# Contexts of a second attention formed transposed on four column groups, in a kernel of two gated layers

## What is computed

```python
x = x + tanh(g_xattn[0]) * L0_xattn(ctx, norm(x), mask, ...)    # 16 heads of 64, over 77 + 128 keys
x = x + tanh(g_ffn[0])   * L0_ffn(norm(x), ...)                 # 128 -> 512, butterflies, gelu, 512 -> 128
x = x + tanh(g_xattn[1]) * L1_xattn(norm(x), ctx, ...)          # 16 heads of 8, the 32 best of 77 keys
x = x + tanh(g_ffn[1])   * L1_ffn(norm(x), ...)                 # 8 experts, the best one for each token
```

```python
scores = einsum('bhsd,bhnd->bhsn', Q, K) / SCALE
topk_scores, topk_indices = top_k(scores, 32)
weights = softmax(topk_scores)
context = einsum('bhsk,bhskd->bhsd', weights, selected V)       # 8 values a head, 16 heads
out = context @ Wo.T + bo
```

## Time and profile before

| | us |
|---|---|
| median of 3 executions | 827.6 |
| lowest and highest | 823.84, 827.65 |
| the profiled execution | 824.25 |
| its span, first to last instruction | 822.5 |
| busy in the span: PE, DVE, ACT, POOL | 727.6, 594.8, 460.3, 453.1 |

### The profile page before, as it was taken

How to read it: one execution, slowest core, us unless ns; L and a number is a source line. 1 busy time by engine, 2 the same in 40 slices (tenths; PEclk the granted TensorE clock), 3 DMA queues, 4 the chain that set the end, 5 groups by cost and what they waited for, 6 DMA issues and landing times.

```text
span 822.5 us, 17993 instructions
## 1 busy us (share of the span) xinstructions
PE 727.6 (88%) x4442; PEld 579.1 (70%) x4442; DVE 594.8 (72%) x3758; ACT 460.3 (56%) x1226; POOL 453.1 (55%) x705
## 2 busy tenths in 40 slices
PE   6789989799999999999999999999999967763796
PEld 5556666677777777777777777777776845552696
DVE  2745435678888888888888888888887888994132
ACT  2265557476858575767676676758575724221231
POOL 6265735755556565655657565656575544653144
PEclk9899999999999999999999999999999965555799
DMA  7200099910000000000000000000000000100772
GB/s 190 60 1 1 8 313 310 293 51 1 1 2 1 0 0 0 0 0 0 0 0 0 0 0 0 0 0 0 0 1 1 2 0 1 39 33 33 202 217 78
DMA packets 38531, 37.85 MB, mean 46 GB/s; under 512 B 3632, under 2 KB 34247, under 8 KB 38482
## 3 DMA queue, kind: packets, MB, share of 16 engines
q1 hardware_dynamic: 32984, 27.76, 12.3%
q10 hardware_dynamic: 3994, 6.36, 2.6%
q0 software_dynamic: 1504, 3.17, 1.1%
HBM read 16.28 MB, written 21.45 MB: 46 GB/s over the span
## 4 chain that ended last, share of the span: by engine, by line
PE 51%; DVE 23%; issue 9%; POOL 6%; ACT 5%; SPq 3%; DMA 2%; DVEq 0%; another core or an unknown queue 0%; POOLq 0%; ACTq 0%
DVE raw L1533 9%; PE bank L850 9%; PE bank L722 8%; DVE m L1527 6%; PE bank L877 4%; PE bank L867 4%; PE bank L868 4%; PE bank L838 4%; PE bank L919 3%; PE bank L936 3%; DVE negmax L1475 3%; PE bank L1156 3%; PE bank L1166 2%; ACT prob L1184 2%; PE bank L899 2%
## 5 line engine op out<-in xcount | busy, mean ns | idle before, releaser
L1533 DVE MATCH_REPLACE8 raw<-m,raw 128x77 f32<-128x77 f32 x1024 | 220.0, 222 | 0.0
L1527 DVE MAX8 m<-raw 128x8 f32<-128x77 f32 x1024 | 189.1, 225 | 1.1 <-DVE raw L1533 0.6
L1184 ACT ACTIVATE prob<-bank,negmax 128x205 f32<-128x205 f32 x256 | 108.3, 428 | 129.1 <-DVE negmax L1475 128.7
L514 POOL TENSOR_TENSOR raw<-raw,m 128x616 f32<-128x616 f32 x64 | 77.9, 1217 | 143.4 <-DVEq L1509 143.4
L495 POOL TENSOR_TENSOR prob<-prob,inv 128x820 f32<-128x820 f32 x64 | 99.4, 1554 | 72.6 <-DVE inv L1480 72.6
L850 PE MATMUL bank<-kvT,g_sb 128*128 128x205 f32 x512 | 123.4, 364 | 0.0
L1475 DVE TENSOR_REDUCE negmax<-bank 128x2 f32<-128x410 f32 x128 | 74.0, 578 | 50.6 <-PE bank L850 49.6
L850 PEld LDWEIGHTS bank<-kvT,g_sb 128*128 128x128 f32 x512 | 82.6, 189 | 10.1
L936 PEld LDWEIGHTS bank<-v,p1T 77*128 77x128 f32 x512 | 75.1, 217 | 15.1 <-issue 4.7
L936 PE MATMUL bank<-v,p1T 77*128 (+1 forms) x512 | 72.4, 269 | 8.1 <-ACT p1T L1184 3.9
L1533 DVE MATCH_VALUE_LOAD raw<-m,raw 128x8 f32 x1024 | 77.7, 76 | 0.0
(11 more groups left out here) (232 smaller groups left out, 1347.6 us busy)
## 6 DMA issues: line engine op xcount, KB each, us to landing
z_sorted<-no_row SPq DMA_DIRECT2D x1, 17415.0 KB, 64.4
b_w<-in_L_ffn_W ACTq DMA_DIRECT2D x23, 256.0 KB, 3.2
z_tile<-z_sorted SPq DMA_DIRECT2D x23, 129.0 KB, 3.2
w<-in_L_ffn_W SPq DMA_DIRECT2D x8, 256.0 KB, 4.6
raw<-in_L_xattn_Wkv SPq DMA_DIRECT2D x2, 512.0 KB, 5.5
xs<-in_x SPq DMA_DIRECT2D x1, 960.0 KB, 6.9
cx<-in_ctx SPq DMA_DIRECT2D x1, 577.5 KB
raw<-in_L_xattn_Wq SPq DMA_DIRECT2D x1, 512.0 KB, 3.7
```

Source lines behind the costliest of these rows:

```text
L1184: return nc.scalar.activation(dst, src, f, **kw)
L1527: v.max(m8[:, h, r, :], sw[:, h, src, :]).then_inc(s[name], 1)
L1533: v.match_replace(sw[:, h, 1, :], m8[:, h, r, :], sw[:, h, src, :], TAKEN)\
```

## The change

The values are held without the column of ones; for each batch GpSimd (`widen_values`, slot 4) copies them into `v_wide`, in which a block of 32 columns holds the 8 values of one head and zeros. The contexts of a batch are formed all at once, in slot 1 of E, and transposed: the weights are 32 columns of v_wide or of `ones_wide`, the moving operand is p1T of one head (now kept for all 16), and head 4j + q is summed into the rows 32j to 32j + 31 of the result (its own 8 rows there, zeros in the others), by the j-th group of 32 columns of TensorE. The ones give the sums, spread over the same rows. So 32 products of 32 weight columns and 128 moving columns take the place of 16 of 128 weight columns and 9 moving ones, and c_zT comes from VectorE directly: the reciprocal is of 128x128, and context_T with its copy is gone. Users of bank X stand further apart in slots 3 to 5 of TensorE and ScalarE. spread_keys goes from slot 0 to slot 2 of GpSimd, and the last roots are taken in three parts, in slot 6 of step 2 and slots 2 and 6 of step 3. TensorE's loop starts at step 5.

```diff
 k1T = sb("k1T", [128, NB, NK])
-v1 = sb("v1", [NK, NB, H, D1 + 1])
+v1 = sb("v1", [NK, NB, H, D1])
+v_wide = sb("v_wide", [NK, QUADS * (128 + D1)])
+ones_wide = sb("ones_wide", [NK, QUADS, 32])
 wr = sb("wr", [128, NE])
...
 m8 = sb("m8", [128, H, ROUNDS, 8])
-p1T = sb("p1T", [NK, 4, 128])
-c_inv = sb("c_inv", [128, H])
-c_z = sb("c_z", [128, H, D1])
+c_inv = sb("c_inv", [128, 128])
 c_zT = sb("c_zT", [128, 128])
...
-z_tile = flat("z_tile", RING * ROW).rearrange("p (u w) -> p u w", u=RING)
+z_flat = flat("z_tile", RING * ROW)
+z_tile = z_flat.rearrange("p (u w) -> p u w", u=RING)
+p1T = z_flat[0:NK, 2 * ROW:2 * ROW + H * 128].rearrange("p (h q) -> p h q", h=H)
 bf_rows = z_tile[0:2 * PST * HC, 0, 0:256]
...
            topk_done=8, sub_done=4, e_done=4, p1_ready=4, p1T_psum=4, p1T_ready=4,
-           ctx_psum=4, cinv_ready=1, cz_ready=1, cT_psum=1, cT_ready=1, o1_psum=1, xo_added=1,
+           ctx_psum=1, vw_ready=1, cinv_ready=1, cz_ready=1, o1_psum=1, xo_added=1,
            x3_ready=1, c_stats=2, c_eps=1, crs_ready=1, rz_ready=1, rz_kept=1, rT_psum=1, rT_ready=1,
...
     g.iota(token_no[:, :], pattern=[[128, NB]], base=0, channel_multiplier=1).then_inc(s["c_token"], 1)
-    g.memset(v1[:, :, :, D1:D1 + 1], 1.0).then_inc(s["c_const"], 1)
-    pool.wait_ge(s["c_const"], 6 + NE)
+    for w in (v_wide[:, :], ones_wide[:, :, :]):
+        g.memset(w, 0.0).then_inc(s["c_const"], 1)
+    pool.wait_ge(s["c_const"], 7 + NE)
+    for q in range(QUADS):
+        g.memset(ones_wide[:, q, D1 * q:D1 * q + D1], 1.0).then_inc(s["c_const"], 1)
     g.affine_select(out=ident[:, :], in_=ident[:, :], compare_op=ALU.not_equal, fill=1.0, base=0,
...
-    def roots(b0, b1):
+    def roots(b0, b1, parts=(0, 1, 2)):
...
         rx, rx2, rc, exponent = (a[:, b0:b1] for a in (rs_x, rs_x2, rs_c, half))
-        pool.wait_ge(s["st_x"], 2 if b1 == 1 else 2 * NB)
-        then(g.tensor_scalar(rx, var_x, EPS, 1.0, ALU.add, ALU.mult))
-        then(g.tensor_tensor(rx, rx, exponent, ALU.pow))
-        then(g.tensor_tensor(rx2, rx, rx, ALU.mult))
-        then(g.tensor_tensor(rx2, rx2, var_x, ALU.mult))
-        then(g.tensor_scalar(rx2, rx2, EPS, 1.0, ALU.add, ALU.mult))
-        pool.wait_ge(s["st_c"], 2 if b1 == 1 else 2 * NB)
-        then(g.tensor_scalar(rc, var_c, EPS, 1.0, ALU.add, ALU.mult))
-        then(g.tensor_tensor(rc, rc, exponent[0:NK, :], ALU.pow))
-        then(g.tensor_tensor(rx2, rx2, exponent, ALU.pow))
-        then(g.tensor_tensor(rx, rx, rx2, ALU.mult))
+        if 0 in parts:
+            pool.wait_ge(s["st_x"], 2 if b1 == 1 else 2 * NB)
+            then(g.tensor_scalar(rx, var_x, EPS, 1.0, ALU.add, ALU.mult))
+            then(g.tensor_tensor(rx, rx, exponent, ALU.pow))
+        if 1 in parts:
+            then(g.tensor_tensor(rx2, rx, rx, ALU.mult))
+            then(g.tensor_tensor(rx2, rx2, var_x, ALU.mult))
+            then(g.tensor_scalar(rx2, rx2, EPS, 1.0, ALU.add, ALU.mult))
+            then(g.tensor_tensor(rx2, rx2, exponent, ALU.pow))
+            then(g.tensor_tensor(rx, rx, rx2, ALU.mult))
+        if 2 in parts:
+            pool.wait_ge(s["st_c"], 2 if b1 == 1 else 2 * NB)
+            then(g.tensor_scalar(rc, var_c, EPS, 1.0, ALU.add, ALU.mult))
+            then(g.tensor_tensor(rc, rc, exponent[0:NK, :], ALU.pow))
...
                         ALU.mult).then_inc(s["kbd_ready"], 1)
+
+    def widen_values(b):
+        reach(pool, "ctx_psum", b, 0)
+        w = v_wide[:, :].rearrange("p (q r) -> p q r", q=QUADS)[:, :, 0:128]
+        g.tensor_copy(w.rearrange("p q (j w) -> p q j w", j=4)[:, :, :, 0:D1],
+                      batch(v1.rearrange("p b h d -> p b (h d)"), b).rearrange("p (j q d) -> p q j d", q=QUADS, j=4))\
+            .then_inc(s["vw_ready"], 1)
...
                     rsqrt(B, b_mv, b_rs, "b_stats", "b_eps", "brs_ready")
-                    spread_keys(B)
             if slot == 1:
...
                     copy_keys(A)
+                if B is not None:
+                    spread_keys(B)
             if slot == 3:
...
                     keep_top(C, 2)
+                    widen_values(C)
                 if P is not None:
...
                 roots(1, 4)
-            if (i, slot) == (3, 6):
-                roots(4, NB)
+            if (i, slot) in ((2, 6), (3, 2), (3, 6)):
+                roots(4, NB, {(2, 6): (0,), (3, 2): (1,), (3, 6): (2,)}[i, slot])
             if slot == 5:
...
-    def contexts(b, q):
+    def contexts(b):
         free("M")
-        reach(pe, "p1T_ready", b, q + 1)
-        for n in range(4):
-            c = CT0 + (4 * q + n) * (D1 + 1)
-            last = mm(M[:, c:c + D1 + 1], p1T[:, n, :], v1[:, bass.ds(b, 1), 4 * q + n, :].squeeze(1),
-                      start=True, stop=True)
+        reach(pe, "p1T_ready", b, QUADS)
+        reach(pe, "vw_ready", b, 1)
+        for q in range(QUADS):
+            for n in range(2):
+                for j in range(4):
+                    w = v_wide[:, 128 * q + 32 * j:128 * q + 32 * j + 32] if n == 0 else ones_wide[:, q, :]
+                    last = mm(M[32 * j:32 * j + 32, CT0 + 128 * n:CT0 + 128 * n + 128], w, p1T[:, 4 * j + q, :],
+                              start=(q == 0 and n == 0), stop=(q == QUADS - 1), skip_group_check=True)
         last.then_inc(s["ctx_psum"], 1)
-        if q == QUADS - 1:
-            read_next("M", "cz_ready", 5, 1)
-
-    def context_T(b):
+        read_next("M", "cz_ready", 5, 1)
+
+    def second_out(b):
         free("M")
         reach(pe, "cz_ready", b, 1)
-        turn(M[:, 0:128], c_z[:, :, :].rearrange("p h d -> p (h d)")).then_inc(s["cT_psum"], 1)
-        read_next("M", "cT_ready", 5, 1)
-
-    def second_out(b):
-        free("M")
-        reach(pe, "cT_ready", b, 1)
         mm(M[:, 0:D], c_zT[:, :], l1_wT[:, 3, :], start=True, stop=True).then_inc(s["o1_psum"], 1)
...
                     scores(A, 2)
-                if C is not None:
-                    contexts(C, 0)
                 if B is not None:
...
                     project_out(A2, 3)
-                if E is not None:
-                    context_T(E)
                 if A is not None:
                     project(A, 2)
-                    probs_T(A, 0)
+                if C is not None:
+                    second_probs_T(C, 1, 4)
                 if E is not None:
...
                 if A is not None:
+                    probs_T(A, 0)
                     scores(A, 3)
-                if C is not None:
-                    second_probs_T(C, 1, 4)
             if slot == 4:
-                if A is not None:
-                    attend(A, 0, 1)
-                if A is not None:
-                    scores(A, 4)
                 if B is not None:
                     second_scores(B, 0)
-                if C is not None:
-                    contexts(C, 1)
+                if A is not None:
+                    attend(A, 0, 1)
+                if A is not None:
+                    scores(A, 4)
                 if B is not None:
...
                     probs_T(A, 1)
+                if C is not None:
+                    second_probs_T(C, 2, 4)
+                if A is not None:
                     project(A, 3)
...
                     ffn_T(A2)
-                if C is not None:
-                    second_probs_T(C, 2, 4)
                 if A is not None:
                     scores(A, 5)
+                if B is not None:
+                    second_scores(B, 2)
                 if E is not None:
                     router_T(E)
-                if B is not None:
-                    second_scores(B, 2)
             if slot == 6:
...
                     scores(A, 6)
-                if C is not None:
-                    contexts(C, 2)
                 if A is not None:
...
                 if E is not None:
-                    if i == 5:
-                        pe.wait_ge(s["ld_router"], 32)
                     logits(E)
...
-    run_steps(pe, step)
+    def before_loop():
+
+        pe.wait_ge(s["ld_router"], 32)
+        free("M")
+        read_next("M", "lg_ready", 6, 2)
+
+    run_steps(pe, step, LAGS - 1, before_loop)
...
             if slot == 3:
-                if E is not None:
-                    move(E, c_zT, "cT_psum", "cT_ready")
                 if A is not None:
                     projected(A, 2)
+                if C is not None:
+                    second_probs_out(C, 1)
+                if A is not None:
                     probs_out(A, 0)
                     exps(A, 3)
-                if C is not None:
-                    second_probs_out(C, 1)
                 if i == 2:
...
             if slot == 4:
-                if A is not None:
-                    attended(A, 0)
                 if B is not None:
                     second_scores_out(B, 0)
+                if A is not None:
+                    attended(A, 0)
                 if C is not None:
...
                     probs_out(A, 1)
+                if C is not None:
```

(49 more changed lines are left out.)

## The result

| | before | after |
|---|---|---|
| median, us (4 executions each) | 825.8 | 835.8 |
| lowest to highest | 823.8 to 827.7 | 833.8 to 837.3 |
| the profiled execution, its span | 824.25, 822.5 | 834.4, 832.5 |
| TensorE busy in the span | 727.6 | 703.0 |
| loop step, down to down | 38.78 | 39.66, but 41.2 in four of ten |

The account below looks back on a forecast made before the run. TensorE and VectorE were taken to bound the kernel in turn, VectorE pacing slots 0 to 4. 11 x 1.1 - 3.5 - 2 - 1 + 1.5 = +7 on 824.25 gave 831; forecast 833 us, range 829 to 843.

Parts of the forecast that it names:

- Spreading to slot 2: GpSimd's product moved away from b_z: b_z falls from 2.28 to 0.34 us, first maxima start 1.2 us earlier.
- Contexts: TensorE, slot 1: 64 records on four column groups take 2.1 us, between 1.8 and 7.1, replacing 3.2.
- rival (b): Weight loads on TensorE are not covered by streaming: contexts take 3.5 us, kernel 855 us; chance 0.12.
- VectorE's wait: Slot 1: VectorE waits 1.1 us for the contexts, where it waited nothing before.
- Reciprocal: On VectorE, grown from 128x16 to 128x128: 953 ns against 240, +0.71 us.
- Maxima of slots 2 and 4: VectorE: slot 2 maxima at 395.3 against 394.67, 0.6 late; slot 4 maxima at 406.0 against 405.44.
- TensorE's wait for the copy of scores (B,1): Ahead of second_probs_T(C,2), TensorE waits 1.2 us for bank X; slot 5 maxima 1.15 late, +1.1 us a step.
- Start, roots, sort step and end: Outside the 11 full steps: first steps -3.5, roots -2, sort constants -1, last step +1.5 us.
- waits 1.2 us: TensorE's forecast wait ahead of second_probs_T(C,2) for ScalarE to free bank X, if today's place is kept.
- my number stands: If b_z stays slow, maxima 1 at 390.8 still come before the contexts end, so the forecast is unchanged.
- wherever it is earlier, it waits longer: If second_probs_T(C,2) stands earlier in TensorE's order than today, its wait for bank X exceeds 1.2 us.
- Rival (a): TensorE's saving survives, 2.5 us a step, if maxima 4 come some 2.5 us earlier: 794 to 820; chance 0.25.

Follow-up runs that it names:

- e6: Changed kernel with all 32 context products written to rows 0 to 31, through one column group: 918.3 us, one execution.
- e4: Changed kernel with ScalarE's copy of second_scores(B,1) placed ahead of the slot 4 exponentials: 812.6 us, ratio 0.983 to the kernel before.
- e1: Kernel before with only spread_keys moved from slot 0 to slot 2: 803.6 us, ratio 0.973 to the kernel before.
- e7: Kernel before with spread_keys in slot 2 and the last roots in three parts: 801.3 us, ratio 0.967 to the kernel before.
- e8: Changed kernel with four unused products (0.9 us) ahead of second_probs_T(C,2) in TensorE's slot 5: 830.4 us, ratio 1.001 to the kernel before.
- e3: Changed kernel with second_probs_T(C,2) and its copy put back behind project(A,3) and the turn of f_z: 824.6 us, ratio 0.994.
- e2: Changed kernel with spread_keys put back in slot 0: 841.0 us, ratio 1.016 to the kernel before.
- e5: Changed kernel with a reciprocal of 16 columns, not 128, spread by broadcasting: 825.4 us, ratio 0.995 to the kernel before.

## Why the prediction was right

The forecast, 833, is 2.8 us from the measured 835.8, and its working can be taken term by term. The closeness of the absolute number flatters it: against the 827.6 known then it says +5.4 and its sum says +7, and the change measured is +10.

- **Spreading to slot 2:** b_z at 0.34 forecast, 0.35 measured; the first maxima 1.2 earlier, measured 1.24. GpSimd's product and the operations behind it in slot 2 leave no slack, as the step said: the timeline of GpSimd has

```profile
398.33 2.27 POOL L516 TENSOR_TENSOR wT<-k1T,head_mask 128x1232 f32<-128x1232 f32 x1
400.56 1.21 POOL L530 TENSOR_TENSOR raw<-raw,m 128x616 f32<-128x616 f32 x1
401.94 0.19 POOL L510 TENSOR_SCALAR f_rs<-f_mv 128x1 f32<-128x1 f32 x1 [0.17 <-DVE f_mv L1507]
```

  with below_max, which starts right behind the product, over at 401.77, and only 0.17 us of idle time before the root of f_z.
- **Contexts:** 2.1 us with two changes of shape forecast; 1.89 measured and 0.1 ahead of it, near the lower bound of 1.8. The four column groups do run side by side (e6: 7.10 on one), and the 64 loads are hidden: 16 turns of 0.11 us are 1.8 already. The page "TensorE: Matmul & The Clock Gate" of the Trainium skill ("The mechanism") says that weight loads overlap running matmuls only for another row group; the 1.89 us, with all weights in the same rows, do not agree, and rival (b) falls with it. The factor is 3.8 for four groups, where the 2.38 of the same page of the Trainium skill ("Measured speedup vs the span model") for three gave an estimate of 3.2.
- **VectorE's wait:** 1.1 forecast, 0.88 measured (the 0.2 of the contexts). **Reciprocal:** 953 ns forecast, 957 measured. **Maxima of slots 2 and 4:** 395.3 and 406.0 forecast, 395.12 and 405.89 measured.
- **TensorE's wait for the copy of scores (B,1):** 1.2 forecast, 1.27 measured, and e4 shows that it is this wait, for it goes with the order on ScalarE and takes the step along. Maxima of slot 5 at 410.6 forecast, 410.64 measured. The step: 39.9 forecast, 39.66 measured, +0.9 and not +1.1, since the waits of slots 6 and 7 gave some back.
- **Start, roots, sort step and end:** -5.5, -1 and +1.5 forecast; -6.0, and together -1.3 - 1.3 + 1.7 + 0.8 = -0.1 measured. That -5.5 comes close is luck in its parts: in the first two steps the spreading gives 2.3 (e1), not 3.5, and the roots 3.3 (e7), not 2, and the changed kernel was 0.7 ahead at the first down, which no term had.

**What failed** is smaller. The sum had no term for the clock: the step "waits 1.2 us" counted the wait alone, and in four of ten steps the clock came down and cost another 1.55 us each, 6.2 us in all. Half of it was covered by luck, by terms that erred the other way (11 times 0.2 in the loop, 0.5 at the start, 0.6 around the sort, 3.3 in all); so a sum of +7.1 stands against a measured +10. A filler, one copy moved or the turn put back takes it away (e8, e4, e3). The statement "my number stands", should b_z stay slow, is right for the loop (+0.26 a step) and wrong for the start and the end, where e2's trace is 8.5 us later. And I counted one new wait where slots 4 and 5 have three: those of 0.53 and 0.61 replace saved work and cost nothing more, since the maxima of slot 5 come where the sum had them, but the step "wherever it is earlier, it waits longer" did not name them.

**Rival (a)** did not come true: its 2.4 to 2.5 us of TensorE's saving are in the trace to a tenth, but its condition, maxima 4 earlier by 2.5, was not met. With the copy moved (e4) the kernel is 1.7% faster than before, inside that rival's range; but e4 is slower than e1, which has the moved call and none of TensorE's saving, so e4's gain doesn't show that the saving survives. What decides between e4 and the changed kernel is ScalarE's order in slot 4, which no step of mine named as something that could be changed at no cost.

**What stays open:** how much the filler is worth (4 to 9 us, by the figure taken); and why only four steps of ten fall to the lower clock, with the same waits in all ten. Three of ten in e5, two in e6 and one in e2 have it, with the same wait of 1.3 us in every step, and none in e3, e4 and e8, where that wait is gone or 0.3 to 0.4; each count is from one execution.

## What to carry to other kernels

Look first for the engine whose queue passes everything on: here a wait or a longer instruction on VectorE in slot 1 went into the step nearly whole (e5, e6), and one in slot 0 did so only as long as no later wait took it up (e1 against e2), while TensorE's saving only turned into waits. When an engine is relieved, list what it will reach too early, and ask of each whether the copy that it waits for is queued behind something that needn't come first; moving one copy of 0.43 us was worth 23 us. Take a change of several parts apart before judging it: the one call moved in e1 gains 2.7%, and the whole loses 1.2%.

## What the runs showed of the hardware

- **Column groups:** float32 products of 32 weight columns by 128 moving columns on four column groups need 1.89 us for 64 records, 0.030 a record, against 7.10 on one group. Weight loads are hidden in both.
- **The clock** fell to its lower level behind three waits of 0.53, 0.61 and 1.27 us in slots 4 and 5, in four of ten steps, and in none of ten with 0.9 us of useless products in the last one. More work on TensorE was faster.
- **VectorE beside GpSimd:** a 128x128 tensor_scalar takes 0.35 us alone and 2.28 when GpSimd's product of 2.27 us starts just before it. The page "SBUF — State Buffer" of the Trainium skill ("Who interferes with whom") says that a VectorE instruction in a two-port mode and a GpSimd one share a pair of ports under an exclusive lock, held for the whole instruction by whichever issues first; the 2.28 us agree with that, since b_z ends 0.09 us behind GpSimd's product (387.62 against 387.53 in the earlier trace rows).
